# When GpSimd issues the gathers of the image rotation: fewer in the last four slots of the attention ahead, one more behind each image's slopes

## What is computed

```python
x = x + causal_attention(per_subject_linear(x))          # 16 heads of 64
x = x + local_transformer(rigid_transform(x, dx, angle)) # 6 layers
x = x + gated_linear_attention(diffusion(x))
x = x + moe_ffn(expert_mix(x))

# rigid_transform: each of the 16 "images" x[b] is 128 x 128
xp = c * gx - s * gy + dx[:, 0];  yp = s * gx + c * gy + dx[:, 1]
ix, iy = grid positions of xp, yp;  wx1 = ix - floor(ix);  wy1 = iy - floor(iy)
out = gather(iy0, ix0) * wy0 * wx0 + gather(iy0, ix1) * wy0 * wx1 \
    + gather(iy1, ix0) * wy1 * wx0 + gather(iy1, ix1) * wy1 * wx1   # bilinear, 0 outside
```

## Time and profile before

| | |
|---|---|
| time, median of 3 runs | 2627.02 us (2624.55 to 2627.31) |
| the profiled execution | 2627.24 us, its span 2625.4 us |
| busy of that span | PE 94%, DVE 76%, ACT 72%, POOL 67% |
| causal attention and ahead | 0 to 296 us |
| rotation | 296 to 552 us |
| local layers and the rest | 552 to 2625 us |

### The profile page before, as it was taken

One profiled execution on the slowest core, in us unless ns is written; L12 is line 12 of the kernel. 1 busy time (PEld: TensorE's weight loads), 2 busy tenths in 40 slices (PEclk: granted clock), 3 DMA queues, 4 the chain that ended last, 5 costly groups with the idle time before them and its releaser, 6 DMA issues.

```text
span 2625.4 us, 98068 instructions
## 1 busy us (share of the span) xinstructions
PE 2457.4 (94%) x36441; PEld 1721.1 (66%) x36441; DVE 2001.0 (76%) x4387; ACT 1889.6 (72%) x6630; POOL 1761.6 (67%) x1605
## 2 busy tenths in 40 slices
PE   6999799978999999999999999999999999789999
PEld 5888454545666666666666666666666666468884
DVE  5555499976888888888888888888888888565544
ACT  4777588856788888878888888888788888533323
POOL 1788766547788888878888888887878887312200
PEclk8999799989999999999999999999999999899999
DMA  4101200021111111121112111211112111100000
GB/s 118 15 15 15 49 12 11 11 70 29 31 33 50 47 41 34 32 64 40 33 33 61 39 39 33 56 41 41 33 40 57 41 33 33 36 1 1 1 1 16
DMA packets 176292, 91.06 MB, mean 35 GB/s; under 512 B 40926, under 2 KB 172232, under 8 KB 175824
## 3 DMA queue, kind: packets, MB, share of 16 engines
q1 hardware_dynamic: 167200, 80.50, 11.4%
q0 software_dynamic: 8192, 4.21, 1.4%
q10 hardware_dynamic: 432, 0.07, 0.0%
HBM read 30.57 MB, written 3.76 MB: 13 GB/s over the span
## 4 chain that ended last, share of the span: by engine, by line
DMA 28%; PE 26%; SPq 24%; DVE 9%; issue 6%; POOL 5%; ACT 1%; another core or an unknown queue 1%; DVEq 0%; POOLq 0%; ACTq 0%
DMA rg_prod<-vt 26%; SPq L556 23%; DVE rg_prod L952 3%; POOL rs L1549 2%; PE scores L654 2%; PE bank L1114 2%; PE bank L626 1%; PE bank L1847 1%; PE bank L1871 1%; POOL t_pair L1539 1%; PE bank L2104 1%; PE bank L1841 1%; PE bank L1865 1%; PE bank L1131 1%; PE bank L675 1%
## 5 line engine op out<-in xcount | busy, mean ns | idle before, releaser
L1549 POOL TENSOR_TENSOR rs<-ssc,neg_half 128x8 f32<-128x8 f32 x384 | 647.5, 1686 | 43.5 <-DVE ssc L1370 43.5
L1477 ACT ACTIVATE pr<-scores,negmax 128x64 f32<-128x64 f32 x1536 | 461.7, 313 | 59.9 <-DVE negmax L1378 34.1
L1539 POOL TENSOR_TENSOR t_pair<-qn_pair,tabs 128x512 f32<-128x512 f32 x384 | 489.2, 1274 | 13.1 <-DVE qn_pair L1358 12.5
L1529 POOL TENSOR_TENSOR pr<-pr,rec 128x256 f32<-128x256 f32 x384 | 235.7, 614 | 314.4 <-DVE rec L1350 314.2
L1114 PE MATMUL bank<-wqk,xs 128*128 128x512 f32 x768 | 407.1, 612 | 22.8 <-DVE qn_pair L1358 19.2
L1013 POOL DMA_INDIRECT rg_win<-rg_images,share_down x256 | 250.4, 978 | 117.9 <-DVE rg_prod L952 61.9
L1477 ACT ACTIVATION_READ_ACCUMULATOR pr<-scores,negmax 128x1 f32 x1536 | 311.5, 203 | 0.0
L1468 ACT COPY vt<-bank 128x256 f32<-128x256 f32 x361 | 135.1, 374 | 208.9 <-issue 113.5
L1366 DVE TENSOR_REDUCE ss<-sq 128x8 f32<-128x512 f32 x384 | 261.1, 680 | 31.9 <-ACT sq L1500 30.8
L1358 DVE TENSOR_TENSOR qn_pair<-bank,rs 128x512 f32<-128x512 f32 x384 | 257.7, 671 | 29.3 <-POOL rs L1549 29.0
L1131 PE MATMUL bank<-oT,wo 128*128 128x128 f32 x1536 | 266.7, 296 | 0.0
(11 more groups left out here) (307 smaller groups left out, 5541.9 us busy)
## 6 DMA issues: line engine op xcount, KB each, us to landing
rg_prod<-vt SPq DMA_DIRECT2D x1536, 32.0 KB
wqk<-in_L_ffn_Wqkv SPq DMA_DIRECT2D x20, 256.0 KB
rg_win<-rg_images,share_down POOLq DMA_INDIRECT x256
wv<-in_L_ffn_Wqkv SPq DMA_DIRECT2D x20, 128.0 KB
wo<-in_L_ffn_Wo SPq DMA_DIRECT2D x20, 128.0 KB
w<-in_L_ffn_W SPq DMA_DIRECT2D x6, 341.0 KB
rg_images<-rg_prod SPq DMA_DIRECT2D x1, 1625.0 KB, 8.9
rg_images<-XT SPq DMA_DIRECT2D x16, 64.0 KB
```

The source lines that it names most:

```text
L1477: ex = act.activation(pr[t % 2][:, h * BAND:(h + 1) * BAND], sl_ps[:, h // 2, h % 2 * BAND:(h % 2 + 1) * BAND], ACT.Exp, bias=negmax[t % 2 ...
L1539: pool.tensor_tensor(t2[t % 2][:, :].rearrange("p (i h f e) -> p i h f e", i=2, h=GH, f=2), qn[t % 2][:, :].rearrange("p (i h f e) -> p i ...
L1549: pool.tensor_tensor(rs[t % 2][:, :], ssc[t % 2][:, :], neg_half[:, 0:8], ALU.pow)\
```

## The change

```diff
@@ pool_images
                 if u >= FIRST_GATHER:
-                    for n in range(2 + (u % GROUPS == 0) + 2 * (u >= TICKS + 2)):
+                    for n in range(2 + (u % GROUPS == 0 and u < TICKS + 2)):
                         pool_gather(pool, done)
                         done += 1
@@ the 64 steps
                 if step == 1 and SLOPES <= b + SLOPES - 1 < B:
                     pool_slopes(pool, b + SLOPES - 1)
+                    if done < B * RG_GROUPS:
+                        pool_gather(pool, done)
+                        done += 1
```

## The result

| | time (us) | TensorE clock, mean |
|---|---|---|
| kernel before, median of 4 runs (lowest, highest) | 2627.16 (2624.55, 2633.41) | |
| changed kernel, median of 4 runs | 2654.39 (2652.32, 2657.16) | |
| ratio after / before | 1.0095, 95% interval 1.0080 to 1.0111 | |
| profiled execution before / after | 2627.24 / 2654.07 | 0.979 / 0.972 |
| its span before / after | 2625.4 / 2652.3 | |

The change makes the kernel 27 us slower. The profiled execution is 0.3 us from the median, so its trace may stand for it. Here is the table of windows of the changed kernel: the seam, then two stretches of the rotation, then two microseconds inside the first of these (columns: window, its length, busy us and count of TensorE, its weight loads, VectorE, ScalarE and GpSimd; granted clock; DMA share; GB/s).

The account below looks back on a forecast made before the run. Rotation taken as bound by VectorE, the seam by TensorE's signals coming late behind GpSimd's gathers. 2627.2 - 9 (seam) + 12.8 (images) + 0.45 (gathers moved into the rotation) = 2631.5 us, range 2614 to 2648.

Parts of the forecast that it names:

- What bounds the kernel: Rotation proper bound by VectorE, 3.618 us a step; seam before it bound by something else, with TensorE's second cut finishing late.
- The rest of the kernel: From the end of the rotation on: must take the same 2073 us as before.
- The seam, -9 us: Between first attention and rotation: nine fewer gathers bring the second product 7.7 us earlier and save 1.4 us of colliding additions.
- The choice of 3.3 us: At the seam: allowance from the end of GpSimd's gathers at 302.2 to the second product at 305.5, not a reading.
- rival d: At the seam: SP's weight loads, not gathers, delay the signals, so no gain there; 2639 us, chance 0.13.
- the 4.8 us of slow steps: Four steps after the seam's second product: 19.3 us where 14.5 would do; only 1.4 us counted as gained.
- The images, +12.8 us: In the rotation: five gathers in a row behind slopes cost 0.7 us for the first image, 1.1 for each of 11 others.
- TensorE runs freely for some 2.9 us of such a run: In the images: TensorE slows only after 2.9 us of five gathers in a row, leaving a slow part of 3.2 us.
- The row that was called the closest: Kernel before, rotation from 437.41 us: six gathers nearly in a row cost 4.1 us over twelve steps.
- Rival (c), the clock: In the images: the clock falls in each run of five gathers, some 2 us more per image; 2655.5 us, chance 0.17.
- Rival (b), the lead holds: In the images: TensorE wins back in other steps what it loses in the run, no cost; 2618.7 us, chance 0.25.
- Rival (e), neither: Seam and images: neither the nine nor the twelve gathers matter to TensorE; 2626.3 us, chance 0.10.

Follow-up runs that it names:

- h2_ahead: Changed kernel with the third gather ahead of the slopes, not behind them, on chip 5: 2647.89 us, 1.0043 of the kernel before.
- f1_plain: Changed kernel with GpSimd issuing plain copies in place of gathers in the rotation, rotated images left out, on chip 3: 2606.97 us, 0.9923 of the kernel before.
- e2_images: Kernel before with its run of 17 gathers at the seam, plus the third gather behind each slopes, on chip 2: 2602.79 us, 1.0006 of the kernel before.
- e3_ahead: Changed kernel with the third gather ahead of the slopes, not behind them, on chip 2: 2605.34 us, 1.0012 of the kernel before.
- e4_busy: Kernel before with an unused 128x400 addition by GpSimd behind each slopes, on chip 2: 2614.26 us, 1.0060 of the kernel before.
- f2_sp: Changed kernel with SyncE issuing plain copies in place of the rotation's gathers, rotated images left out, on chip 3: 2615.49 us, 0.9947 of the kernel before.
- f3_split: Kernel before with each step's second gather released by the step's second product, on chip 3: 2633.00 us, 1.0014 of the kernel before.
- g2_ahead: Changed kernel with the third gather ahead of the slopes, not behind them, on chip 6: 2606.49 us, 1.0014 of the kernel before.
- f4_quarter: Changed kernel with a quarter of the placing's matmuls, images incomplete, on chip 3: 2626.34 us, 0.9988 of the kernel before.

## Why the prediction was right or wrong, point by point

The forecast of 2631.5 us missed and so did the range, which ended at 2648. The direction (slower) was the one forecast, if only by 4 us, and the runs of five gathers behind the slopes are what costs. The step that failed is their price: 1.1 us an image, because the slow part of a run was put at 3.2 us and the fall of the clock at nothing. Measured were 3.4 us an image.

- **What bounds the kernel**: right. The rest of the kernel moved by 1.8 us only.
- **The seam, -9 us**: the sign and the place were right, measured -12.4. The run ends at 301.50 (302.2 said), the slopes at 303.86 (304.6). The choice of 3.3 us between the run's end and the second product was too careful: TensorE's loads flow 1.2 us after it, and the second product is at about 302.8, not 305.5, so that it comes 10.4 us earlier and not 7.7. The doubt that SP's weight loads share the blame (rival d) falls: they ran as before, and the wait ended with the gathers. Of the 4.8 us of slow steps behind it 2.1 went (17.2 us to step 4 for 19.3), where 1.4 were counted.
- **The images, +12.8 us**: this term failed, measured +41.3. The list of GpSimd came out as worked out, five in a row behind each slopes. Two sizes were off. First, "TensorE runs freely for some 2.9 us of such a run" was taken from the six-gather run; here the loads slow down 1.8 to 2.1 us after the first gather (344.0 to 344.3 against 342.24). Second, the run lasts 6.5 us and not 6.1: the fourth and fifth gathers took 1.23 and 1.19 us. So the slow part is at least 4.5 us and not 3.2. In the prediction's own terms, the placing made VectorE wait about 1.7 us in each of the 12 images, where 0.7 was worked out, and the cut about 1.7 us where it was late, not 0.4. The row that was called the closest, six gathers for 4.1 us, was read as one delay; step by step it is 2.2 us right behind the run and about 1 us at the first step of each of the next two images. That was a sign that a spent lead goes on costing.
- **Rival (c), the clock**: right, given 0.17, in that the clock fell in the images. It forecast 2655.5; the profiled run took 2654.07. Its price per image was 1.1 + 2 = 3.1 us, measured 3.4. That the total came within 1.4 us is partly luck: the seam gave 3.4 us more than it counted, the images took 4.1 us more, and the rest 2.0 us less. How much of the 3.4 us is the clock and how much the slow issue, no run parts. That the kernel before had shown the fall once already, in a run of gathers a little longer, should have weighed more than a reading, to the half microsecond, of when a run begins to bite. Two prices of 1.1 and 3.1 us per image that hang on a length read from a single run are not known apart, and the dearer one belonged inside the range. Nor can the fall be tied to a run of five: in h2_ahead the clock fell behind a run of three.
- **Rival (b), the lead holds**: wrong on this chip. By the prediction's own rate (2.7 us behind in 3.2 us) 4.5 us of slow issue make 3.8 us, still inside the lead of 4.2, and yet VectorE waited 1.64 us for the cut in the image shown above. Whether that rate or that lead was sized wrong, the rows don't tell.
- **Rival (e), neither**: wrong on the chip on record, 5 and 14, and right on chips 2 and 6, where each half of the change is worth 0.3% or less. The rule behind it, that DMA and compute don't disturb each other in SBUF (the Trainium skill, SBUF — State Buffer, section SBUF: two separate sides), isn't refuted: the plain copies of f1_plain bear it out, and the hold-up goes with GpSimd's indirect instruction, not with the transfer. The reading "gathers hold up TensorE" was right, but rival (e) was argued about the wrong part of a gather.
- **The rest of the kernel**: 2071 us behind the rotation's last move, 2073 said.

## What to carry to other kernels

Where an off-path engine issues work that slows the bottleneck's supplier, don't ask whether it has room but how long its runs get: on the chip on record two gathers a step cost nothing as long as TensorE had its lead, five in a row 3.4 us, because a lead is a finite buffer, and behind the run the clock falls as well. An added item does its harm where it closes the gap between two pairs. An item that is only moved can do it elsewhere: in seven of the kernels (e2_images, e3_ahead, e4_busy, f2_sp, f3_split, g2_ahead, h2_ahead) GpSimd's slopes came to meet VectorE's additions, for up to about 1 us an image. And before a change is kept for a gain of half a per cent, time it on several chips: here the same edit was worth 1.6% on one and nothing on another.

## What the runs showed of the hardware that was not expected

- **The chips differ in one behaviour.** With the same kernel before, chips 2 and 6 take 2602.58 and 2600.03 us, chips 3, 5 and 14 take 2630 to 2640, and the traces place most of the difference in the rotation: on the first two TensorE's loads are never held up by gathers (e2_images), in every trace of the others and of the chip on record they are. No chip came twice (that of the result on record is not numbered), so that it is the chip and not something else that differs from group to group is likely and not shown. What inside the chip differs is open.
- **It goes with the indirect instruction.** Plain copies of the same size and number, by GpSimd or by SyncE, leave TensorE's 32 loads in one piece of 1.45 us. How GpSimd's resolving of indices reaches TensorE's issue is not known from these runs; TensorE shows no semaphore and no other wait in the pauses, and it loses less when it has fewer small instructions to get through (f4_quarter). The large matmuls of the slots ahead of the rotation were not looked at for it.
- **The clock falls late.** In the changed kernel it is 1.00 while the loads dribble, and 0.50 in 350 to 352 us, when the gathers of the run are over and TensorE is busy throughout. In the longer run at the seam of the kernel before it was 0.50 with gathers still going out. The windows just ahead of 350 us in the changed kernel:

```profile
344.00:346.00 2.00, 1.82 (x15) 0.44 (x10) 1.89 (x5) 1.76 (x3) 1.44 (x2) 1.00 0.09 12
346.00:348.00 2.00, 1.10 (x8) 0.33 (x9) 1.81 (x5) 0.12 (x1) 1.65 (x2) 1.00 0.11 11
348.00:350.00 2.00, 1.83 (x21) 0.95 (x24) 0.41 (x1) 0.32 (x1) 0.77 (x1) 0.84 0.13 14
```
